# Attention results that are no longer turned, and softmax sums from probabilities that VectorE adds up first

## The reference

```python
def attention(x, kv_d_w, q_d_w, k_u_w, v_u_w, q_u_w, rope_k_w, rope_q_w, o_w):
    ...
    v = (kv_d @ v_u_w).reshape(b, s, NH, HD)
    ...
    scores = jnp.einsum('bqhd,bkhd->bhqk', q, k) * scale
    causal = jnp.tril(jnp.ones((s, s), dtype=bool))
    scores = jnp.where(causal[None, None], scores, jnp.finfo(scores.dtype).min)
    probs = jax.nn.softmax(scores, axis=-1)
    out = jnp.einsum('bhqk,bkhd->bqhd', probs, v).reshape(b, s, H)
    return out @ o_w
```

## Time and profile before

| what | value |
|---|---|
| median of three runs | 2880.9 us |
| the profiled execution: time, span | 2877.17 us, 2875.4 us |
| busy over the span | PE 2312.7 us (80%), DVE 1395.9 us (49%), POOL 27%, ACT 23% |
| granted clock of PE over the span, of 1 | 0.899 |
| L2631, weights of 64 columns, 512-column form | 32.1 us busy, mean 624 ns, x128 |
| L2643, turns of results | 18.2 us busy, mean 289 ns, x128 |

### The profile page before, as it was taken

The page is one execution under the profiler, slowest core; times in us unless marked ns, Lnnn a source line. Parts: engine busy times, 40 slices in busy tenths (PEclk is TensorE's granted clock), DMA queues, the critical chain, the costliest instruction groups (busy, mean ns, idle before and its releaser), DMA issues. The chain is left out here.

```text
span 2875.4 us, 30303 instructions
## 1 busy us (share of the span) xinstructions
PE 2312.7 (80%) x9850; PEld 1094.5 (38%) x9853; DVE 1395.9 (49%) x3223; ACT 651.8 (23%) x1134; POOL 766.4 (27%) x1108
## 2 busy tenths in 40 slices
PE   8999972886999998748999984369999953799980
PEld 3344331444544443314444441123444423445440
DVE  4987762332722222836666663844554423422226
...
GB/s 236 14 38 88 37 0 99 72 82 165 104 23 243 254 251 184 175 174 110 77 104 93 110 50 118 49 118 2 1 16 16 2 94 247 43 26 91 92 80 164
DMA packets 124334, 283.35 MB, mean 99 GB/s; under 512 B 20015, under 2 KB 44335, under 8 KB 117040
## 3 DMA queue, kind: packets, MB, share of 16 engines
...
## 5 line engine op out<-in xcount | busy, mean ns | idle before, releaser
L1904 DVE CUSTOM_DVE_ANT_0 D_scores<-D_ps,D_mask 128x256 f32<-128x256 f32 (+1 forms) x512 | 174.0, 387 | 79.1 <-PE D_ps L1800 75.7
L1651 POOL TENSOR_SCALAR_AFFINE_SELECT D_probs<-D_probs 128x256 f32<-128x256 f32 x256 | 106.4, 421 | 296.3 <-ACT D_probs L1709 296.1
L1709 ACT ACTIVATE D_probs<-D_ps 128x512 f32<-128x512 f32 (+1 forms) x256 | 125.3, 543 | 158.3 <-PE D_ps L1822 158.3
L2715 DVE TENSOR_REDUCE F_neg_max<-F_ps 128x4 f32<-128x2048 f32 (+1 forms) x64 | 94.0, 1489 | 132.9 <-PE F_ps L2599 132.9
L1181 PE MATMUL C_ps<-C_down_shared,C_hs 128*128 128x512 f32 x256 | 120.8, 622 | 27.2 <-DVE C_hs L1345 14.7
L3232 PE MATMUL G_ps<-G_gate_up,G_xgT 128*128 x304 | 138.5, 599 | 0.0
L1169 PE MATMUL C_ps<-C_xT,C_gate_shared 128*128 128x512 f32 x256 | 115.4, 594 | 0.6 <-ACT C_xT L1044 0.6
L1169 PE MATMUL C_ps<-C_xT,C_up_shared 128*128 128x512 f32 x256 | 115.1, 592 | 0.0
L297 PE MATMUL A_ps<-A_wo,A_h 128*128 128x512 f32 x160 | 87.1, 696 | 34.7 <-DVE A_h L407 34.7
L2416 POOL TENSOR_SCALAR_AFFINE_SELECT F_probs<-F_probs 128x512 f32<-128x512 f32 x64 | 42.8, 680 | 265.8 <-ACT F_probs L2493 265.8
L2493 ACT ACTIVATE F_probs<-F_ps 128x1536 f32<-128x1536 f32 (+1 forms) x48 | 76.4, 1591 | 153.1 <-PE F_ps L2615 153.1
...
...
(9 more groups left out here) (426 smaller groups left out, 4656.1 us busy)
## 6 DMA issues: line engine op xcount, KB each, us to landing
...
```

Source lines behind the costliest of these rows:

```text
L1651: last = nc.gpsimd.affine_select(now[:, :, 0:P], now[:, :, 0:P], [[0, 2], [1, P]], ALU.is_ge, 0.0, base=0, channel_multiplier=-1)
L1709: nc.scalar.activation(probs[at % 2][:, 2 * pair:2 * pair + 2, 0:w], ps[:, 4 + unit % 3, :].rearrange("p (h q) -> p h q", h=2)[:, :, 0:w], ...
L1904: last = nc.vector.tensor_tensor_reduce(scores[:, u % 2, h, first:256], ps[:, 2 + u % 2, h * 256 + first:(h + 1) * 256], mask32[:, 0, 0, f ...
L2715: last = nc.vector.tensor_reduce(neg_max[n % 2][:, :, t], ps[:, 0:GROUP, at:at + w], AX_X, ALU.max, negate=True)
```

## The change

- `v` has the 32 columns of each head alone, with neither the one nor the zeros. `times_v` writes four heads side by side into bank 4: per key block four matmuls with 32-column weights instead of four with 64.
- DVE adds up the probabilities over the key blocks into `added` (`add_first_probs` at place 7, `add_last_probs` at place 11). `sums` on PE then multiplies `added` with 32 columns of ones, four heads side by side into bank 5, so that the sum of a head stands in each of its 32 rows, in the same place as its result.
- `keep_oT` on DVE (place 1 of the next `i`) takes the reciprocal of the whole bank, 512 per partition, and multiplies bank 4 with it straight into `oT`, which the output product reads. `keep_pv`, `turn_pv`, `keep_o`, `turn_o` and ACT's copy of it are gone.
- The exponentials wait for the adds that read the same probabilities. POOL no longer clears `v`. Of the rule that holds pieces back, the part for chunk 12 is dropped, and for the last `i` it holds two places instead of four.

```diff
-            return [("turn_o", 4 * b - 4 + t) for t in range(4)] + [("out", 4 * b - 4 + t) for t in range(4)]
+            return [("out", 4 * b - 4 + t) for t in range(4)]
         if k == 0:
-            return (front(b + 1) if ahead else []) + ([("turn_o", 4 * b - 4 + t) for t in range(4)] if b else [])
+            return front(b + 1) if ahead else []
...
-            if i in (CHUNKS - GROUP, CHUNKS) and at < 4:
+            if i == CHUNKS and at < 2:
...
-        v = [sb(f"v{j}", [P, 4, NH, 2 * HD]) for j in (0, 1)]
+        v, ones32 = [sb(f"v{j}", [P, 4, D]) for j in (0, 1)], sb("ones32", [P, ROWS])
...
-        pv, rden = [sb(f"pv{p}", [P, S]) for p in (0, 1)], [sb(f"rden{p}", [P, 4, 2]) for p in (0, 1)]
-        o, oT = sb("o", [P, 4, D]), [sb(f"oT{t}", [P, KD, P]) for t in range(4)]
+        added = sb("added", [P, GROUP, S])
+        rden, oT = sb("rden", [P, S]), [sb(f"oT{j}", [P, GROUP, S]) for j in (0, 1)]
...
-            for j in (0, 1):
-                steps.after(nc.gpsimd.memset(v[j][:].rearrange("p t h e -> p (t h e)"), 0.0))
-                nc.gpsimd.memset(v[j][:, :, :, HD:HD + 1], 1.0).then_inc(v_cleared, 1)
+            nc.gpsimd.memset(ones32[:], 1.0).then_inc(presets, 1)
...
-                if b < 2:
-                    act.wait_ge(v_cleared, b + 1)
-                else:
-
-                    act.wait_ge(pv_in_psum, 2 * GROUP * (b - 1))
-                nc.scalar.copy(v[b % 2][:, t, :, 0:HD], bank_of("values", n).rearrange("p (h e) -> p h e", h=NH)).then_inc(v_ready, 1)
-
-            def keep_oT(n):
-                act.wait_ge(o_turned, n + 1)
-                nc.scalar.copy(oT[n % 4][:], bank_of("turn_o", n).rearrange("p (k m) -> p k m", k=KD)).then_inc(oT_ready, 1)
+                if b >= 2:
+
+                    act.wait_ge(probs_read, 3 * GROUP * (b - 1))
+                nc.scalar.copy(v[b % 2][:, t, :], bank_of("values", n)).then_inc(v_ready, 1)
...
-                if n and u < 2:
-
-                    act.wait_ge(probs_read, 2 * n + u - 1)
-                elif n:
-                    act.wait_ge(pv_in_psum, 2 * n)
+                if n:
+
+                    act.wait_ge(probs_read, 3 * n + u - 2)
+                    act.wait_ge(added_last if u == 2 else added_first, n)
...
-                elif kind == "turn_o":
-                    pe.wait_ge(o_ready, 2 * GROUP * (b + 1))
-                    for c in range(KD):
-                        last = nc.tensor.transpose(bank[:, c * P:(c + 1) * P], o[:, t, c * P:(c + 1) * P], ident[:])
-                    last.then_inc(o_turned, 1)
                 elif kind == "out":
                     if k == 0:
-                        pe.wait_ge(oT_ready, n + 1)
+                        pe.wait_ge(oT_ready, GROUP * (b + 1))
                         pe.wait_ge(wo_in, 16)
-                    last = nc.tensor.matmul(bank, oT[t][:, k, :], wo[:, k, :], start=(k == 0), stop=(k == KD - 1))
+                    last = nc.tensor.matmul(bank, oT[b % 2][:, k, t * P:(t + 1) * P], wo[:, k, :], start=(k == 0), stop=(k == KD - 1))
...
-                        pe.wait_ge(o_ready, 2 * n)
-                for pair in (0, 1):
-                    for kb, at, w in KEYS[u]:
-                        for h in (0, 1):
-                            r = 2 * pair + h
-                            last = nc.tensor.matmul(ps[h * 2 * HD:(h + 1) * 2 * HD, 4 + pair, kb * P:S],
-                                                    v[b % 2][:, kb, c * GROUP + r, :], probs[u][:, r, at:at + w], start=(u == 0), stop=True,
-                                                    skip_group_check=True)
-                    if u == 2:
-                        last.then_inc(pv_in_psum, 1)
-                    elif pair == 1:
-                        last.then_inc(probs_read, 1)
-
-            def turn_pv(n):
-                for pair in (0, 1):
-                    pe.wait_ge(pv_ready, 2 * n + pair + 1)
-                    for t in range(4):
-                        last = nc.tensor.transpose(ps[:, 4 + pair, t * P:(t + 1) * P], pv[pair][:, t * P:(t + 1) * P], ident[:])
-                    last.then_inc(pv_turned, 1)
+                        pe.wait_ge(oT_ready, n)
+                for kb, at, w in KEYS[u]:
+                    for r in range(GROUP):
+                        head = (c * GROUP + r) * HD
+                        last = nc.tensor.matmul(ps[r * ROWS:(r + 1) * ROWS, 4, kb * P:S], v[b % 2][:, kb, head:head + HD],
+                                                probs[u][:, r, at:at + w], start=(u == 0), stop=True, skip_group_check=True)
+                last.then_inc(probs_read, 1)
+
+            def sums(n):
+                pe.wait_ge(added_last, n + 1)
+                if n:
+
+                    pe.wait_ge(oT_ready, n)
+                for r in range(GROUP):
+                    last = nc.tensor.matmul(ps[r * ROWS:(r + 1) * ROWS, 5, :], ones32[:], added[:, r, :], start=True, stop=True,
+                                            skip_group_check=True)
+                last.then_inc(sums_in_psum, 1)
...
-                        turn_pv(i - 1)
+                        sums(i - 1)
...
-            def keep_pv(n):
-                for pair in (0, 1):
-                    dve.wait_ge(pv_in_psum, 2 * n + pair + 1)
-                    nc.vector.tensor_copy(pv[pair][:], ps[:, 4 + pair, :]).then_inc(pv_ready, 1)
-
-            def keep_o(n):
+            def add_first_probs(n):
+                dve.wait_ge(cut_ready, 3 * n + 2)
+                nc.vector.tensor_copy(added[:, :, 0:P], probs[0][:, :, 0:P])
+                nc.vector.tensor_tensor(added[:, :, P:S], probs[0][:, :, P:S], probs[1][:], ALU.add).then_inc(added_first, 1)
+
+            def add_last_probs(n):
+                dve.wait_ge(cut_ready, 3 * n + 3)
+                dve.wait_ge(added_first, n + 1)
+                steps.after(nc.vector.tensor_tensor(added[:, :, 2 * P:S], added[:, :, 2 * P:S], probs[2][:, :, 0:2 * P], ALU.add))
+                nc.vector.tensor_tensor(added[:, :, 3 * P:S], added[:, :, 3 * P:S], probs[2][:, :, 2 * P:3 * P], ALU.add
+                                        ).then_inc(added_last, 1)
+
+            def keep_oT(n):
                 b, c = divmod(n, GROUP)
-                if c == 0 and b:
-
-                    dve.wait_ge(o_turned, 4 * b)
-                for pair in (0, 1):
-                    dve.wait_ge(pv_turned, 2 * n + pair + 1)
-                    turned = ps[:, 4 + pair, :].rearrange("p (t h e) -> p t h e", t=4, h=2)
-                    steps.after(nc.vector.reciprocal(rden[pair][:], turned[:, :, :, HD]))
-                    at = (c * GROUP + 2 * pair) * HD
-                    nc.vector.tensor_tensor(o[:, :, at:at + 2 * HD].rearrange("p t (h e) -> p t h e", h=2),
-                                            turned[:, :, :, 0:HD], rden[pair][:].unsqueeze(3).to_broadcast([P, 4, 2, HD]), ALU.mult
-                                            ).then_inc(o_ready, 1)
+                dve.wait_ge(sums_in_psum, n + 1)
+                steps.after(nc.vector.reciprocal(rden[:], ps[:, 5, :]))
+                nc.vector.tensor_tensor(oT[b % 2][:, c, :], ps[:, 4, :], rden[:], ALU.mult).then_inc(oT_ready, 1)
...
-                    if s == 0 and 0 <= i - 1 < CHUNKS:
-                        keep_pv(i - 1)
...
-                        if at == 0 and 0 <= i - 1 < CHUNKS:
-                            keep_o(i - 1)
+                        if at == 1 and 0 <= i - 1 < CHUNKS:
+                            keep_oT(i - 1)
+                        if at == 7 and 0 <= i < CHUNKS:
+                            add_first_probs(i)
+                        if at == 11 and 0 <= i < CHUNKS:
+                            add_last_probs(i)
```

More of the change, by code:

```diff
@@ L2255, in pieces_of @@
         return KD if kind in ("low", "out") or (kind == "rope" and n % 2) else 1
-    COST = {"turn_x": 0.44, "turn_o": 0.44}
+    COST = {"turn_x": 0.44}
     pieces_at, done_at, order = {}, {}, []
@@ L2388, in _ @@
         def _(pool):
-            steps = Steps(pool, pool_step)
             pool.dma_start(x[0][:], x5[0:S, :].rearrange("(t p) n -> p t n", p=P)).then_inc(x_in[0], 16)
@@ L2500, in _ @@
                     for at in (2 * s, 2 * s + 1):
-                        for kind, n in done(i, at, 0, "turn_x", "low", "rope", "nope", "values", "turn_o", "turn_m"):
+                        for kind, n in done(i, at, 0, "turn_x", "low", "rope", "nope", "values", "turn_m"):
                             if kind == "turn_x":
@@ L2511, in _ @@
                                 keep_v(n)
-                            elif kind == "turn_o":
-                                keep_oT(n)
                             else:
@@ L2591, in scores_for_max @@
                     if n == 0:
-                        pe.wait_ge(presets, 3)
+                        pe.wait_ge(presets, 4)
                 for t, at, w in SEEN[u]:
```

14 lines of the change are left out of this document (6 added, 8 removed).

## The result

The kernel after takes 2904.0 us (median of five runs, 2894.1 to 2905.2), the kernel before in the same comparison 2881.6 us (2880.4 to 2884.7): ratio 1.0077, 95% interval [1.0057, 1.0097]. The profiled execution takes 2901.2 us at a span of 2899.5 us, against the forecast's 2892 for it. The change made the kernel slower, by 22.4 us where 14.8 were forecast. Of the five runs after, the shortest (2894.1) has a mean granted clock of 0.892, the others 0.887 to 0.889, so part of the cost changes from one execution to the next.

What follows compares the result with a forecast made beforehand. PE was taken to bound the attention stage, with DVE's reciprocal deciding after the change. Chunk terms of +7.8 us and +7 for the clock, together +14.8 on 2880.9, gave about 2896 us, range 2868 to 2924.

Steps and rivals of the forecast that it cites:

- What PE is spared: Attention stage: shorter times_v and dropped turns, less the new sums, shrink PE's work by 37.9 us.
- What DVE gets: Attention stage: adds and a 3.35 us reciprocal give DVE 5.5 us more per chunk, 89 over the stage.
- The walk of quarter 1: Chunk 9: times_v waits 1.2 us for oT, then PE 0.8 for the maximum; second scores start 1.25 later.
- the knee: Reciprocal's length in chunks with pieces: below about 2 us PE decides; at 3.35 times_v waits 1.2 us.
- The loaded chunks: Chunks with pieces, quarters by chunk number modulo 4: quarter 0 -4.4 us each, 1 +1.4, 2 +0.7, 3 +1.3; chunk 0 -1.4.
- The unloaded chunks and the clock: Chunks with few pieces: 2, 12, 13 +2.5 us each, chunk 15 and end +0.3; lower PE clock +7.
- the forecast's +0.3: Chunk 15 and the end: reciprocal and wait for the last adds against dropped turns and four turn_o, +0.3 us.
- The forecast's own ground: Chunks 12 and 13: PE busy only about 12.5 of 22 us, so its clock falls, 2.5 us each.
- Rival 1: At keep_oT: PE decides everywhere if the reciprocal takes 0.7 us; 30 us faster, 2851 us; chance 0.15.
- Rival 2: Chunks with pieces: stalls half as long, PE's clock stays; about 2881 us, no change; chance 0.20.
- Rival 3: Chunks with pieces: PE's clock falls there too, eight falls at 3.5 us; 2924 us; chance 0.15.
- The waits ahead of times_v for oT: First times_v of a chunk: about 1.2 us with pieces, 3 in chunks 12 and 13, 16 to 25 in all.

Runs made afterwards that it cites:

- e1: Kernel after with the reciprocal taken of 8 columns instead of 512, so results are not divided by their sums: ratio 0.9951 to the kernel before, stage 395.6 us.
- e2: Kernel after with the three additions of probabilities replaced by copies of a few columns: ratio 1.0038 to the kernel before, stage 432.1 us.
- e8: Kernel after with the reciprocal taken of 256 columns instead of 512: stage 404.8 us, against 436.0 in the kernel after.
- e5: Kernel after with sums right behind the chunk's third times_v, keep_oT behind its last maximum, the second pair of additions dropped: ratio 0.9960 to the kernel before.
- e7: Kernel after with keep_oT moved behind the next maximum (place 3) and the last pieces held four places: stage 521.7 us, against 436.0 in the kernel after.
- e6: Kernel after with early sums and reciprocal in DVE's gap, plus 22 unread filling products: ratio 0.9934 to the kernel before, in a second run 0.9923.
- e4: Kernel after with ACT copying bank 4 away, reciprocal and multiplication behind the next maximum, last pieces held four places: ratio 0.9997 to the kernel before.
- e3: Kernel after with 22 unread filling products in chunks 2, 12, 15 and before the last output products: ratio 1.0028 to the kernel before.
- e9: Kernel before with unread filling products in chunks 2 and 15 and ahead of the last turns, last pieces held two places: ratio 0.9998 to the kernel before.

## Why the prediction was right, and where a size was off

- **What PE is spared: right.** Times_v over 512 columns steps 1.00 us (2215.21 to 2216.21 in e1), over 384 0.78 (2192.41 to 2193.19), as forecast 1.00 and 0.79. In chunk 8 PE's busy time falls by 4.0 us, in quarters 1 to 3 by 1.6 (1.93). That PE's total falls by 17.1 instead of 37.9 us is for the most part the clock: in the stage (19.1 us less), chunks 0, 1, 3 to 11 and 14, at 0.99 to 1.00, give 24.4 us, and chunks 2, 12, 13 and 15 take 5.3 more than before.
- **What DVE gets: right.** Reciprocal 3.357 us (taken 3.35), adds 1.74, 1.22 and 0.69 (1.76, 1.23, 0.69), copy 0.41 (0.43). Reading from PSUM adds nothing to the long reciprocal, so the row of the same operation and size was the one to go by. DVE's busy times by quarter are 14.2, 20.0, 16.2 and 24.7 us, forecast 14.3, 20.2, 16.3 and 24.9.
- **The walk of quarter 1: right.** From the sums to the second scores it gave 7.05 us; measured 6.93 (2178.71 to 2185.64). The waits are 1.14 and 0.51 us (1.2 and 0.8). That the adds are hidden is shown by e2, the reciprocal's part by e1, the knee by e8, the place by e5 and e7.
- **The loaded chunks: right.** Quarter 0 -4.7 (forecast -4.4), quarter 1 +1.2 (+1.4), quarter 2 +1.0 (+0.7), quarter 3 +1.4, and +1.1 in chunk 11 (+1.3), chunk 0 -1.2 (-1.4), chunk 1 +1.8 (+1.4). Chunks 0, 1 and 3 to 11 together give -0.7 us, and so did the forecast.
- **The unloaded chunks and the clock: the mis-sized term.** For chunks 2, 12 to 15 and the end the forecast has 7.5 + 0.7 + 0.3 + 7 = 15.5 us, measured 25.0: 5.4, 6.6, 5.0, 0.3 and 7.7. Chunk 2 was booked at +2.5 without a further fall, though the rows already had it at 0.78; it went to 0.53 and cost 2.9 more. The end was booked at 2.3: the last products alone take 16.2 instead of 14.0 us, and chunk 15 runs at 0.57, with waits of 4.3 us ahead of times_v and of the output products; the forecast's +0.3 weighs one reciprocal, that of the end, and chunk 15, as empty of pieces as chunk 12, has one at its head too. Chunk 12 took 6.6 for 5.0. That is the whole error of 9.5 us in the profiled execution. Where PE idles ahead of and in chunk 2, and in chunk 12:

```profile
1987.79 1.18 PE L2593 MATMUL F_ps<-F_qT,F_kT 32*128 32x512 f32 x8 [3.21 <-DVE F_neg_max L2695]
...
1990.97 1.94 PE L2622 MATMUL F_ps<-F_added,F_ones 128*32 128x512 f32 x8 [1.57 <-DVE F_added L2713]
...
1997.20 1.94 PE L2612 MATMUL F_ps<-F_probs,F_v 128*32 128x512 f32 x8 [2.16 <-DVE F_oT L2720]
...
2264.38 1.14 PE L2612 MATMUL F_ps<-F_probs,F_v 128*32 128x512 f32 x8 [2.63 <-DVE F_oT L2720]
2265.96 1.66 PE L2593 MATMUL F_ps<-F_qT,F_kT 32*128 32x384 f32 x8 [0.43 <-DVE F_neg_max L2695]
```

  The steps of one shape give the clock away: 1.94 against 1.07 us. In chunk 12 it falls right behind the wait for oT. That this wait is the cause is not shown: in e1, without it, the clock falls in chunk 12 as low (0.70). The forecast's own ground, PE busy about 12.5 of 22 us, fits that better than the single wait.
- **Rival 1** (PE decides): refuted by the reciprocal's row, and its price with it: with almost no reciprocal e1 wins 16 us and not 30. Only with the clock kept does a kernel come nearer, e6 with 22. **Rival 2** (stalls half as long): refuted by quarters 1 to 3. **Rival 3** (the clock falls in loaded chunks): refuted for this kernel, 1.00 in all of chunks 3 to 11 with waits of 1.1 us, but its mechanism is real, as e7 shows with waits of 5.0 us and e4 with one of 3.4. The wait ahead of the fall in chunk 2 of the kernel before, which the prediction takes for one of 0.8 to 1.2 us, was 2.0 (1984.79).

The waits ahead of times_v for oT sum to 23.3 us, where 16 to 25 were forecast. The warning of the Trainium skill (TensorEngine Tiling (Array Packing), Performance Considerations) that a tiled product can leave the copies out of PSUM as the bottleneck agrees with the trace in part. What reads PSUM behind the product does decide, but it is one reciprocal of 3.36 us at its place and not the amount of copying: DVE is busy 272 of 436 us of the stage, and e5 makes the same reads without the loss in the loaded chunks. By the rule of the Trainium skill on the clock (TensorE: Matmul & The Clock Gate, Part 1: The HAM clock gate), that the full clock must be kept up by activity, the filling should help where PE idles and not elsewhere; that agrees with e3 and e6 (10.9 and 15.8 us of stage), with chunk 12 of e1, where less work was enough for the clock to fall to 0.70, and, for the kernel before, with e9's nothing.

What stays open: how chunk 2's loss divides between the waits, among them 3.2 us at the end of chunk 1, and the missing work (in e5 that wait is 1.7 us, and chunk 2 is at 0.59 all the same); how far the clock of the thin chunks changes between executions; e1 with filling, which would have given the ceiling at a clock of 1.00; and why chunk 13 at 0.86 was hardly helped by e3's filling in chunk 12. In chunk 13 of e3 PE still waits 3.11 us for oT, and the products behind are slow.
